# Edge stage of a graph network kernel: TensorE tells attention and projection results less often, four projection banks, lane and tile sums in one bank

## The reference, cut to what matters

```python
def _L1_gnn_ref(h, edge_index, edge_rel_emb, W1, b1, W2, b2, num_nodes):
    x = h[src] + edge_rel_emb
    hid = jax.nn.relu(x @ W1 + b1)
    msg = hid @ W2 + b2
    agg = jax.ops.segment_sum(msg, dst, num_segments=num_nodes)
    return h + agg

def _L1_mix_ref(x, Wqkv, Wout, gamma):
    qkv = x @ Wqkv
    q, k, v = jnp.split(qkv, 3, axis=-1)
    q, k, v = map(to_heads, (q, k, v))        # 8 heads of 32
    q = jax.nn.softmax(q, axis=-1) * SCALE
    k = jax.nn.softmax(k, axis=2)
    context = jnp.einsum('bhnd,bhne->bhde', k, v)
    out = jnp.einsum('bhde,bhnd->bhne', context, q)
    out = out.transpose(0, 2, 1, 3).reshape(B, N, HEADS * DIM_HEAD)
    out = out @ Wout
    return _layernorm_gamma(out, gamma)
```

## Time and profile before

| | us |
|---|---|
| median of 3 runs | 1403.86 (1401.70 to 1406.04) |
| the profiled execution | 1407.83 |
| its span on the core | 1406.1 |
| edge stage in it, first projection to last tile sum | 597 to 1103 |
| gathers of that stage on POOL (313) | 301.9 busy, from 599.6 to 1090.5 |

### The profile page before, as it was taken

One profiled execution on the slowest core, in us unless ns is written; L12 is line 12 of the kernel. 1 busy time (PEld: TensorE's weight loads), 2 busy tenths in 40 slices (PEclk: granted clock), 3 DMA queues, 4 the chain that ended last, 5 costly groups with the idle time before them and its releaser, 6 DMA issues. The chain is left out here.

```text
span 1406.1 us, 22044 instructions
## 1 busy us (share of the span) xinstructions
PE 1159.4 (82%) x7703; PEld 922.4 (66%) x7703; DVE 650.6 (46%) x1630; ACT 465.7 (33%) x976; POOL 485.8 (35%) x530
## 2 busy tenths in 40 slices
PE   3788998988357778769899998989988889957997
PEld 2688995557256667547777776767766654536886
DVE  6777622878623224724444445443455341252332
ACT  2477702423133333613333333333333243221110
POOL 3000002012055662065566665666666000003442
PEclk9999999998679899979999999999999999977999
DMA  5000003200752225645555555555554074485551
GB/s 127 1 2 2 3 2 92 29 1 1 234 174 75 80 81 128 162 136 150 160 166 159 160 166 161 163 161 165 170 169 139 13 235 124 117 185 182 173 177 54
DMA packets 97270, 164.54 MB, mean 117 GB/s; under 512 B 15633, under 2 KB 59309, under 8 KB 96901
## 3 DMA queue, kind: packets, MB, share of 16 engines
q1 hardware_dynamic: 71669, 89.65, 22.4%
q0 software_dynamic: 25488, 73.39, 17.5%
HBM read 137.36 MB, written 27.63 MB: 117 GB/s over the span
## 5 line engine op out<-in xcount | busy, mean ns | idle before, releaser
L2433 POOL DMA_INDIRECT em_gathered<-edge_table,el_which x313 | 301.9, 964 | 192.1 <-DVE em_hidden L2526 108.9
L2130 PE MATMUL em_projected<-em_w,em_attr 128*128 128x256 f32 x1188 | 279.7, 390 | 17.1 <-DVE em_hidden L2526 8.2
L2130 PEld LDWEIGHTS em_projected<-em_w,em_attr 128*128 128x128 f32 x1188 | 230.7, 196 | 59.1 <-issue 13.4
L2526 DVE TENSOR_TENSOR em_hidden<-em_projected,em_gathered 128x512 f32<-128x512 f32 x149 | 101.7, 684 | 199.0 <-PE em_projected L2130 94.0
L2550 ACT ACTIVATE em_hidden<-em_hidden 128x512 f32<-128x512 f32 (+1 forms) x157 | 98.5, 627 | 257.8 <-DVE em_hidden L2526 208.6
L2957 PE MATMUL oe_banks<-oe_wd,xn_T 128*128 x432 | 99.6, 385 | 0.0
L2871 POOL DMA_INDIRECT oe_hidden<-oe_table,oo_node x27 | 25.9, 959 | 184.7 <-DMA oe_table<-state 132.9
L2957 PEld LDWEIGHTS oe_banks<-oe_wd,xn_T 128*128 128x128 f32 x432 | 81.6, 194 | 10.4
L2900 PE MATMUL oe_banks<-xn_T,oe_w 128*128 128x500 f32 x160 | 71.2, 596 | 1.2 <-DMA oe_b<-in_ffn_b_T 1.2
L669 ACT ACTIVATE nm_adj_T<-nm_banks 125x500 f16<-125x500 f32 x100 | 60.0, 604 | 22.9 <-PE nm_banks L572 19.9
L1886 PE MATMUL mx_banks<-mx_w,mx_answer 128*128 x188 | 52.8, 430 | 16.8 <-issue 11.5
(11 more groups left out here) (515 smaller groups left out, 2290.3 us busy)
## 6 DMA issues: line engine op xcount, KB each, us to landing
em_attr<-in_edge_attr_sets SPq DMA_DIRECT2D x156, 256.0 KB
oe_table<-state SPq DMA_DIRECT2D x20, 448.0 KB
oe_wd<-in_ffn_Wd SPq DMA_DIRECT2D x8, 1024.0 KB, 12.4
em_gathered<-edge_table,el_which POOLq DMA_INDIRECT x313
mx_w<-in_ffn_w SPq DMA_DIRECT2D x16, 256.0 KB
oe_table<-state SPq DMA_DIRECT2D x1, 2248.8 KB
state<-in_x SPq DMA_DIRECT2D x5, 448.0 KB
state<-in_x SPq DMA_DIRECT2D x1, 2240.0 KB
```

The lines of the kernel that those rows point to most:

```text
L2130: last = nc.tensor.matmul(into[:, n * DIM:(n + 1) * DIM], attr[:, i % ATTR_RING, (n * KB + f) * 128:(n * KB + f + 1) * 128], w[:, f, :], s ...
L2433: nc.gpsimd.indirect_dma_start(out=gathered[:, n % GATHERED, :], out_offset=None, in_=edge.table, in_offset=bass.IndirectOffsetOnAxis(ap=l ...
L2526: nc.vector.tensor_tensor(pair_slots(k), ahead[:, 0:width, :], gathered[:, at:at + width, :], ALU.add).then_inc(pre_ready, 1)
```

## The change

- `em_projected` has 4 banks in place of 3. `em_lane_sum` and `em_total` become the two halves of one bank, `em_set_sums`.
- TensorE tells `projected_ready` once for k0 and k1 and once for k2 and k3 (149 times become 79); VectorE and SP wait for these counts.
- In the attention, `q_turned` and `correlated` are gone: one semaphore `stepped` is told behind q and v (L2220), and once behind the last correlation. `k_ready` and `out_ready` are told once for the two node tiles of a step. With the projections, TensorE makes 129 increments fewer.
- `sum_tiles(s - 2)` moves from behind the lane sums of set s to behind its pair k1 (and the attention step there); `keep_tiles(s - 2)` on ScalarE moves from the end of the set to behind its pair k2. `sum_lanes` now also waits for `tile_kept` of all tiles summed so far.

```diff
-    GATHERED, HIDDEN_RING, BANKS = 12, 2, 3
+    GATHERED, HIDDEN_RING, BANKS = 12, 2, 4
...
+    tiles_until = lambda s: len([t for t in range(TILES) if last_set(t) <= s])
...
-        lane_sum = p.ps("em_lane_sum", [128, 512], scope=scope)
-        total = p.ps("em_total", [P, 512], scope=scope)
+        set_sums = p.ps("em_set_sums", [128, 2, DIM], scope=scope)
+        lane_sum, total = set_sums[:, 0], set_sums[:P, 1]
...
-                    sp.wait_ge(projected_ready, i - len(EARLY) - ATTR_RING + 1)
+                    sp.wait_ge(projected_ready, LATER[i - len(EARLY) - ATTR_RING] // 2 + 1)
...
-                                       len(EARLY) + r).then_inc(projected_ready, 1)
...
+                    if k % 2 or k + 1 not in LATER:
+                        last.then_inc(projected_ready, 1)
...
                     if s >= 1:
                         pe.wait_ge(lane_kept, s)
+                    if tiles_until(s - 1):
+                        pe.wait_ge(tile_kept, tiles_until(s - 1))
...
                         if k % SET_PAIRS == 1:
                             attention.tensor(pe, 2 * s)
+                        if s >= 2 and k == pairs_of(s)[:2][-1]:
+                            sum_tiles(s - 2, s - 1)
                     if s >= 1:
                         sum_lanes(s - 1)
-                    if s >= 2:
-                        sum_tiles(s - 2)
...
-                            dve.wait_ge(projected_ready, r + 1)
+                            dve.wait_ge(projected_ready, k // 2 + 1)
...
                             attention.scalar(act, k // 2, k % 2)
+                        if s >= 2 and k == pairs_of(s)[:3][-1]:
+                            keep_tiles(s - 2)
                         if s >= 1 and k == pairs_of(s)[0] + 3:
                             keep_lanes(s - 1)
...
-                    if s >= 2:
-                        keep_tiles(s - 2)
```

In the attention:

```diff
-            last.then_inc(self.q_turned, 1)
...
-            last.then_inc(self.correlated, 1)
+            if n == TILES:
+                last.then_inc(self.stepped, 1)
...
-            last.then_inc(self.qv_ready, 1)
+            last.then_inc(self.stepped, 1)
...
-                dve.wait_ge(self.qv_ready, t + 1)
-                if t >= 1:
-                    dve.wait_ge(self.q_turned, t)
+                dve.wait_ge(self.stepped, t + 1)
...
-                last.then_inc(self.out_ready, 1)
+            last.then_inc(self.out_ready, 1)
```

40 lines of the change are left out of this document (20 added, 20 removed).

## The result

| | before | after |
|---|---|---|
| median of 4 runs each, us | 1402.8 (1399.0 to 1406.0) | 1448.0 (1446.1 to 1448.3) |
| ratio, 95% interval | 1 | 1.0305 (1.0268 to 1.0343) |
| profiled execution, us | 1407.8 | 1448.3 |
| its span, us | 1406.1 | 1446.6 |

The kernel is slower by 45 us in the medians and by 40.5 us in the profiled executions; the forecast had 19, less than half of either. After's profiled execution stands only 0.3 us above its median, before's 5 above this median: that is 4.7 of the 45.

The account below looks back on a forecast made before the run. A gather loop of 12.4 us a set was taken as the bound, TensorE nearly full. Terms of +8.6, -0.5, +9, +1 and +1 us were summed to +19, giving 1427 profiled and 1423 us median; range 1391 to 1450.

Parts of the forecast that it names:

- The new wait: Ahead of tile sets' lane sums, TensorE waits for the copy of the tile sum: 2.1 us, 2.35 with outputs.
- The sum of 30 us: Gross total of the waits for the tile copy ahead of lane sums, 14 times: 30 us.
- The waits for `em_hidden`: Sign of being right: TensorE's bank waits before projections, 0.93 us for k0's bank, are gone with four banks.
- The reading of the twos in the output stretch: Output stretch: second node tile of an even step waits 0.95 us more, ten times; the stretch in all +9 us.
- TensorE's chain: Sets with q and v steps: TensorE's own work and waits become the bound, 26.0 us a couple against 25.05.
- the rival in which it falls: Half clock for 3.4 us after each of the 14 new waits, 1.7 us lost each: 1447 us; chance 0.10.
- The tail: Sets 32 to 39: 11.6 and 8 us a couple fit inside 20 us of gathers, so only +1 us.
- the pace of the loop: Couples of sets 7 and 17: eight gathers, late tells and k0's sum stay the bound, 24.8 us: -0.5 us.
- Set 5: In the keys stretch: four waits of 0.95 us hidden by the gathers, and set 5, together +1 us.
- The twos: Projections told in twos: k2 told 1.73 us later, no added q wait in plain sets; 0.95 us waits with outputs.
- the lane sum covers 1.0 of that, so a plain set still waits 0.8 us, as now: Plain sets: q is ready 1.85 us after k3 is told; the remaining wait for q is some 0.8 us, unchanged.
- The faster rival: Fewer increments between lane sums end late tells, so stalls of the first sets and others go: 1391 us; chance 0.17.

Follow-up runs that it names:

- kernel 6: The kernel after with three projection banks, own banks for lane and tile sums, and each projection told singly: 0.9990 of before on a prompt chip, 1.0002 on a late-tell one.
- kernel 8: The kernel after with four spare matmuls in the wait ahead of lane sums of 13 tile sets: 1379.1 us against 1388.9 for after, same chip.
- the second pair: Traces of the unchanged kernels before and after, taken again on one late-tell chip: 1407.0 and 1440.4 us.
- the twos' kernel: The kernel before with only the projections told in twos: 1.0127 of before on a late-tell chip, 1.0217 on a prompt one.
- kernel 4: The kernel before with only the attention steps' increments merged, 59 of the 129: 0.9992 of before on a late-tell chip.
- kernel 3: The kernel after with each projection told singly, shared bank and four banks kept: 1418.5 us, 1.0044 of before on a late-tell chip.

## Why the prediction was off

- **The new wait** was there as worked out in the sets with attention steps: 2.11 us for 2.1, 2.35 with outputs for 2.35. The sum of 30 us was too low: the 14 waits of the forecast come to 33, mostly by late tells in the tail, and sets 7 and 17, where none was expected, have 1.3 and 2.5. That the profile puts 29.4 us down to the copy is near 30 by chance, as it counts these two and leaves out those of sets 15 and 33. The waits for `em_hidden` ahead of projections are gone. The reading of the twos in the output stretch held too (+7.7 for +9).
- **TensorE's chain** as the new bound held: 25.7 us for a couple where the clock stayed, 26.0 forecast. That the kernel after is bound by it and no longer by the gathers shows in the two kinds of chips: its q stretch takes 254.2 us on one and 252.5 on the other, before's time for it 237 and, in kernel 6, 210. With the clock mended (kernel 8) it takes 244.2, and 237.3 + 8.1 = 245.4 was forecast (with before on the late-tell chip).
- **The step that failed first is the clock.** The sum took the clock as unchanged behind the new waits, since it had stayed at 1.00 behind 1.97 us, and the rival in which it falls got 0.10. Waits of 2.11 us are followed by half clock in 6 of 8 cases in after, and in 5 of 8 on the prompt chip. The rival's price was right (1.7 us; 1.65 measured), its count of 14 too high. It is 5.6 us of the 17.0 in the q stretch on the late-tell chip, 6.6 to 8.2 on the prompt one by kernel 8, and up to 5 more in the tail. Nor do the lengths of the earlier trace rows bound a safe one: waits of 1.89 us are followed by half clock twice in after, one of 2.47 and two of 2.35 us are not. One wait of 1.97 us that left the clock alone was no ground to call 2.1 us safe. Of the 21.5 us between forecast and measurement in the profiled executions the clock makes 6 to 11; 5.3 lie ahead of set 1 and 2.0 behind the lane sums of set 39, and no run puts these on the change.
- **The tail,** +1 forecast, +4.2 and +7.5 measured. I had noted that TensorE's tells come late around runs of gathers, and priced the new wait only with prompt ones; with a late one it is 5.2 and 3.8 us, and the clock is at half behind it.
- **Sets around an early k2.** The sum gave sets 7 and 17 the pace of the loop and took sets 12 and 22 for common plain ones. Behind the lane sums of these two TensorE waits 1.89 us for q, not 0.8: with the tile set after them they take 28.3 us each, before 25.5 and 25.3. That is +5.9 us. In each of these couples the clock falls twice in after (behind the wait ahead of the lane sums of set 11 or 21, and behind the wait for q) and once in before, which is 3.3 of it; the rest had no place in the sum. Set 5, the first with a wait ahead of its lane sums (1.81 us): +4.2 here and +2.5 in the second pair, forecast within +1.
- **The twos** were the change's larger part by themselves, 1.27% on a late-tell chip, where I had 0.64%. The step "the lane sum covers 1.0 of that, so a plain set still waits 0.8 us, as now" is right on its own, but on a late-tell chip the 0.8 before came from late tells and in the twos' kernel from the chain; it hid that k2 had moved. The miss in the q stretch is small there (+2.9 for 0), and is in waits for a bank, which the fourth bank takes away in after; on the prompt chip, without that cover, it is 11.6.
- **The faster rival,** late tells ended by fewer increments, is out: in kernel 4 and in after most tells of this stage are as late as before (numbers below), and the stall at the first sets was not shorter but longer, 13.7 us for 11.1.

The two parts are not additive. In thousandths of before on late-tell chips: the twos alone 13, the shared bank's wait alone 4 (kernel 3, which has the fourth bank as well), both 26 to 31. The twos put the copy behind k3's projection; that makes the wait 2.11 us instead of some 1.3. The clock fell behind six of the eight waits of the first kind and behind none of kernel 3's six of the second.

No version here beats the kernel before. The best, own banks told singly, takes its time.

## What to carry to other kernels

Price a new wait of TensorE with what its clock does behind it: here 2.1 us of waiting cost 1.7 us more in most cases, and filling such waits with useless matmuls gave 10 us back. Before a tell is merged with a later one, list everything that stands behind the earlier one, including copies that free a bank; two waits on one chain cover each other, so that taking away one alone gives back half and shows the other. And measure on more than one chip: stalls of one chip's own can hide part of what a change costs (3.1 and 2.6% here against 5.5).

## What the runs showed of the hardware

**The same kernel takes 1405 us on some chips and 1315 us on others,** 6.5% apart (7 to 25 runs of before each: medians 1409.6 and 1405.6; 1314.7, 1316.0 and 1314.0). What differs in the traces is when TensorE's tells arrive, counted by the semaphore events between 600 and 1000 us against the ends of the matmuls. In the traces from the slower kind some tells have no event (in before about 30 of 250). Of the others most come over 0.3 us late: 154 of 220 in before (the latest 12.0 us), 142 of 210 in before once more, 119 of 162 in kernel 4, 59 of 107 in after (5.2 us). In the ten traces from the faster kind none of 143 to 293 tells is over 0.05 us late, whatever the kernel. VectorE's tells, as far as they have an event, are prompt in both kinds (in before all but 3 of 137). One such place, kernel 6, while the gathers run as in the earlier trace rows:

```profile
744.50 7.07 PE L2130 MATMUL em_projected<-em_w,em_attr 128*128 128x256 f32 x32
...
746.48 0.69 DVE L2527 TENSOR_TENSOR em_hidden<-em_projected,em_gathered 128x512 f32<-128x512 f32 x1 [3.87 <-PE em_projected L2130]
...
748.15 0.69 DVE L2527 TENSOR_TENSOR em_hidden<-em_projected,em_gathered 128x512 f32<-128x512 f32 x1 [0.19 <-PE em_projected L2130]
...
747.44 0.94 POOL L2433 DMA_INDIRECT em_gathered<-edge_table,el_which  x1 [1.51 <-DVE em_hidden L2527]
```

The first pair ends at 746.4, a quarter of the row, and is summed at 746.48; the second at 748.1, and is summed at 748.15, in the middle of a gather. So the "gather loop" of the prediction sets the pace on the late-tell chips only: on the prompt ones two sets take 12.18 + 10.45 us, 22.6, against 25.05. That the late tells make the whole 6.5% is likely and not shown: kernel 6 has a trace of each kind, and of the 86 us between them 37 lie ahead of the lane sums of set 1, mostly where tells were not counted. Why chips differ, and whether fewer or shorter runs of gathers would help on the late-tell kind, no run here settles.

The second surprise is the clock, told above: behind waits of 2.11 us the granted clock fell to half for some 3.4 us in most cases, and four spare matmuls in the wait kept it at full in all 8 of the q and v stretch. It fell behind waits of 1.89 us too, and stayed at full behind some of 2.35 and 2.47; what decides, no run here shows.
